# Routed expert blocks taken two at a time, and one tensor-engine event for each gather: a decoder layer on one Trainium2 core

## What is computed

```python
x = layernorm(x + attn(x))          # a state-space mixer with 32 heads
x = layernorm(x + xattn(x, ids))    # 4 experts, chosen by the token's id
x = layernorm(x + ffn(x))           # this is where the change is

def ffn(x):                         # 16 experts, top 2, and a shared one
    logits = x @ gate_w.T
    top_idx = top_k(logits + expert_bias, 2)
    w = softmax(logits)[top_idx]; w = w / sum(w)
    out = sum_k w_k * swiglu(x, expert top_idx_k)
    return out + swiglu(x, shared)
# swiglu(x, e) = (silu(x @ wg_e.T) * (x @ wu_e.T)) @ wd_e.T, inner width 176
```

## Time and profile before

| | |
|---|---|
| median of 3 runs | 666.92 us (666.61 to 666.98) |
| the profiled execution | 666.86 us |
| its span, first to last instruction | 665.1 us |
| mean granted TensorE clock | 0.985 |
| PE busy | 631.1 us, 95% of the span, 3545 matmuls |
| DVE, POOL, ACT busy | 531.7, 479.6, 453.6 us |
| routed blocks, 566.7 to 641.8 us | PE busy 71.2 us of 75.1 |
| end, 641.8 to 665.1 us | PE busy 4.6 us of 23.3 |

### The profile page before, as it was taken

The page is one execution under the profiler, slowest core; times in us unless marked ns, Lnnn a source line. Parts: engine busy times, 40 slices in busy tenths (PEclk is TensorE's granted clock), DMA queues, the critical chain, the costliest instruction groups (busy, mean ns, idle before and its releaser), DMA issues.

```text
span 665.1 us, 12037 instructions
## 1 busy us (share of the span) xinstructions
PE 631.1 (95%) x3545; PEld 489.1 (74%) x3545; DVE 531.7 (80%) x851; ACT 453.6 (68%) x739; POOL 479.6 (72%) x458
## 2 busy tenths in 40 slices
PE   7989999999999999999999999999999999899961
PEld 6677888888878888788888887878888877444530
DVE  6999999999999999999999999948952658323253
ACT  3769788797887887978879788776423455333534
POOL 4396989879879898798887987596914647854463
PEclk9999999999999999999999999999999999999995
DMA  4261113112121131111211212042063493577443
GB/s 161 88 253 49 65 49 111 63 48 75 42 106 63 48 111 63 48 63 48 111 63 48 88 47 87 0 128 101 16 164 87 109 306 147 156 234 235 100 118 112
DMA packets 25994, 66.67 MB, mean 100 GB/s; under 512 B 4099, under 2 KB 16899, under 8 KB 23179
## 3 DMA queue, kind: packets, MB, share of 16 engines
q1 hardware_dynamic: 23131, 58.54, 26.2%
q0 software_dynamic: 2832, 7.75, 4.4%
HBM read 58.00 MB, written 9.85 MB: 102 GB/s over the span
## 4 chain that ended last, share of the span: by engine, by line
PE 81%; DVE 7%; issue 3%; ACT 3%; POOL 2%; another core or an unknown queue 1%; DMA 1%; POOLq 0%; ACTq 0%; DVEq 0%
PE ps L874 36%; PE ps L888 9%; PE ps L904 7%; PE ps L889 4%; PE ps L1168 4%; DVE conv L1723 4%; PE ps L806 3%; PE ps L824 3%; PE ps L1217 3%; PE ps L848 2%; PE ps L913 1%; PE ps L1142 1%; PE ps L914 1%; PE ps L1192 1%
## 5 line engine op out<-in xcount | busy, mean ns | idle before, releaser
L1723 DVE SCALAR_TENSOR_TENSOR conv<-ps,w_raw,conv 128x506 f32<-128x506 f32 (+3 forms) x352 | 320.5, 933 | 14.8 <-ACT conv L1368 8.4
L874 PE MATMUL ps<-x_hi,w_hi 128*128 128x512 f32 x384 | 158.0, 412 | 2.6 <-DVE x_lo L1644 1.5
L1368 ACT ACTIVATE conv<-ps,w_raw 128x512 f32<-128x512 f32 x160 | 108.4, 688 | 63.7 <-PE ps L874 63.1
L874 PE MATMUL ps<-x_hi,w_lo 128*128 128x512 f32 x384 | 151.3, 394 | 0.0
L874 PE MATMUL ps<-x_lo,w_hi 128*128 128x512 f32 x384 | 150.1, 391 | 0.0
L528 POOL TENSOR_TENSOR decay<-cum_b,cum_tok 128x512 f32<-128x512 f32 (+1 forms) x128 | 103.4, 829 | 9.1 <-DMA cum_b<-cum_scratch 9.1
L874 PEld LDWEIGHTS ps<-x_hi,w_hi 128*128 128x128 f32 x384 | 72.3, 188 | 20.6 <-issue 2.4
L534 POOL TENSOR_TENSOR decay<-decay,mask 128x512 f32<-128x512 f32 x64 | 82.7, 1292 | 5.0
L874 PEld LDWEIGHTS ps<-x_hi,w_lo 128*128 128x128 f32 x384 | 72.1, 188 | 16.8 <-DVE w_lo L1649 0.2
L874 PEld LDWEIGHTS ps<-x_lo,w_hi 128*128 128x128 f32 x384 | 72.4, 189 | 12.7
L1353 ACT ACTIVATE conv<-conv 128x1024 f32<-128x1024 f32 x80 | 79.3, 1059 | 1.5 <-DVE conv L1723 1.5
(11 more groups left out here) (286 smaller groups left out, 1107.7 us busy)
## 6 DMA issues: line engine op xcount, KB each, us to landing
cum_b<-cum_scratch SPq DMA_DIRECT2D x16, 1024.0 KB, 4.6
w_raw<-in_winT SPq DMA_DIRECT2D x15, 778.0 KB, 4.3
y_all<-in_wgu SPq DMA_DIRECT2D x4, 1408.0 KB, 12.8
late<-in_wdn SPq DMA_DIRECT2D x2, 1408.0 KB
x_scratch<-conv SPq DMA_DIRECT2D x19, 128.0 KB, 4.9
late<-in_woutT SPq DMA_DIRECT2D x1, 2048.0 KB, 8.4
ys_scratch<-y_blk SPq DMA_DIRECT2D x32, 64.0 KB
res_scratch<-conv SPq DMA_DIRECT2D x11, 130.0 KB
```

Source lines behind the costliest of these rows:

```text
L874: mm = pe.matmul(ps[:, tile_bank(n, tile) + hf, :], wp[:, par, w], xp[:, kk, t], start=(i == 0), stop=(i == 5))
L1368: act.activation(conv[:, par, tile, hf * 512:(hf + 1) * 512], ps[:, tile_bank(n, tile) + hf, :], ACT.Copy, scale=w_raw[:, par, tap:tap + 1 ...
L1723: dve.scalar_tensor_tensor(out=o[:, :, s:], in0=u[:, :, 0:T - s], scalar=w_raw[:, par, c:c + 1], in1=o[:, :, s:], op0=ALU.mult, op1=ALU.ad ...
```

## The change

- PE takes routed items in pairs (i = 11, 13, ... 33): gate_up(i), gate_up(i + 1), down(i - 2), down(i - 1), turn_block(i + 2), turn_block(i + 3), turn_hidden(i), turn_hidden(i + 1). The first pair is laid out singly, since the shared items end inside it. ACT and DVE follow in the same order.
- POOL gathers the first 4 blocks freely. Of each further pair of blocks, the first waits for gate_up(i) of the pair four blocks earlier, the second for turn_hidden(i + 1) of it; from the second such pair on, one residual gather stands between them and waits for down(i - 2). The residual gathers are so spread over the pairs of blocks 6 to 20.
- The first six row gathers use the same three events in the last two pairs. The other ten wait for no event of PE.
- What hangs on the residual rows moves back with them: `SEEN_AT` by 6 items, `PICK_AT` by 4.
- At the end ACT normalises b = 0 to 4 and DVE b = 5 to 7, each one step behind the statistics of the next block; POOL normalises none. DVE's first weigh steps stand behind the last gate step, no longer between the last ones.

```diff
@@ -60,16 +60,15 @@
 RES = D + 4
-SEEN_AT = TBS + 11
-PICK_AT = TBS + 14
-LAST_ACT, LAST_POOL = 4, 6
+SEEN_AT = TBS + 17
+PICK_AT = TBS + 18
+LAST_ACT = 5
 HOISTED, LEADING = 3, 2
-BESIDE = 19
 PICK_PARTS = ((0, 0, HOISTED), (1, 0, LEADING), (0, HOISTED, TB), (1, LEADING, TB))
...
 NX = 8
-AHEAD = 3
+AHEAD = 4
 NSEL = 2
...
@@ -472,10 +471,8 @@
                     sp.wait_ge(S["n2a"], b + 1)
-                elif b < LAST_POOL:
-                    sp.wait_ge(S["n2p"], b - LAST_ACT + 1)
                 else:
-                    sp.wait_ge(S["n2"], b - LAST_POOL + 1)
+                    sp.wait_ge(S["n2"], b - LAST_ACT + 1)
                 sp.dma_start(out[b * P:(b + 1) * P, :], o_tok[:, b, :]).then_inc(S["st_out"], 16)
@@ -679,8 +676,6 @@
-                if j >= AHEAD:
-                    pool.wait_ge(S["tx_done"], j - AHEAD + 1)
                 pool.indirect_dma_start(xb[:, j % NX, :], None, x2_dram,
@@ -689,7 +684,6 @@
                     pool.wait_ge(S["st_res"], 16 * TBS)
-                    pool.wait_ge(S["gu_done"], TBS)
                 pool.indirect_dma_start(res_tok[:, b, :], None, res_dram,
@@ -716,27 +710,41 @@
             pool.wait_ge(S["v_tab"], 1)
-            for j in range(NBLK):
+            def in_pair(i, place):
...
+                if place == 0:
+                    pool.wait_ge(S["gu_done"], i + 1)
+                elif place == 1:
+                    pool.wait_ge(S["dn_done"], i - 1)
+                else:
+                    pool.wait_ge(S["ht_done"], i + 2)
...
+            for j in range(AHEAD):
                 gather_block(j)
...
                     add_residual(TBS - 4)
-                elif j == 4:
+            for j in range(AHEAD, NBLK, 2):
+                i = TBS + j - AHEAD
+                in_pair(i, 0)
+                gather_block(j)
+                if j == AHEAD:
                     add_residual(TBS - 3)
-                elif j == 5:
+                elif j // 2 - AHEAD // 2 <= TB:
+                    in_pair(i, 1)
+                    gather_res(j // 2 - AHEAD // 2 - 1)
+                in_pair(i, 2)
+                gather_block(j + 1)
+                if j == AHEAD:
                     add_residual(TBS - 2)
                     add_residual(TBS - 1)
-                if 7 <= j < 7 + TB:
-                    gather_res(j - 7)
...
             def beside_blocks(n):
-                j = BESIDE + min(n // 2, (n + 3) // 3)
-                if j < NBLK:
-                    pool.wait_ge(S["gu_done"], TBS + j + 1)
-                else:
-                    pool.wait_ge(S["dn_done"], ITEMS - 1)
+                if n < 6:
+                    in_pair(ITEMS - AHEAD + n // 3 * 2, n % 3)
@@ -752,10 +760,6 @@
                     gather_row(k, b)
-            for b in range(LAST_ACT, LAST_POOL):
-                pool.wait_ge(S["q2"], b + 1)
-                pool.tensor_scalar(o_tok[:, b, :], y_of[:, 0, b, :], ln_m2[:, b, 0:1], ln_v2[:, 1, b:b + 1],
-                                   ALU.subtract, ALU.mult).then_inc(S["n2p"], 1)
@@ -1290,21 +1294,35 @@
             turn_block(TBS)
-            for i in range(TBS, ITEMS + 2):
-                if i < ITEMS:
-                    gate_up(i)
+            for i in range(TBS, ITEMS, 2):
+                gate_up(i)
                 if i == TBS:
...
                     down(TBS - 1)
-                if i - 2 >= TBS:
+                gate_up(i + 1)
+                if i > TBS:
                     down(i - 2)
                 if i + 2 < ITEMS:
-                    turn_block(i + 2)
                     read_expert(i + 2 - TBS)
-                if TBS <= i - 1 < ITEMS:
-                    turn_hidden(i - 1)
+                if i > TBS:
+                    down(i - 1)
+                if i == TBS:
+                    turn_block(TBS + 2)
+                    turn_hidden(TBS)
+                    turn_block(TBS + 3)
+                    turn_hidden(TBS + 1)
+                else:
+                    if i + 2 < ITEMS:
+                        turn_block(i + 2)
+                        turn_block(i + 3)
+                    turn_hidden(i)
+                    turn_hidden(i + 1)
+                if i + 2 < ITEMS:
+                    read_expert(i + 3 - TBS)
+            down(ITEMS - 2)
+            down(ITEMS - 1)
@@ -1598,27 +1616,30 @@
             take_block(TBS)
-            for i in range(TBS, ITEMS + 2):
-                if i < ITEMS:
-                    silu_gate(i)
+            for i in range(TBS, ITEMS, 2):
+                silu_gate(i)
                 if i == TBS:
...
                     take_y(TBS - 1)
-                if i < ITEMS and i - 2 >= TBS:
-                    take_y(i - 2)
-                if i >= ITEMS:
-                    take_hidden(i - 2)
-                    if i == ITEMS:
-                        act.preload_act_table_set("natural_log_exp_and_others")
+                silu_gate(i + 1)
+                if i > TBS:
                     take_y(i - 2)
...
                     take_block(i + 2)
+                    take_block(i + 3)
+                if i > TBS:
+                    take_y(i - 1)
                 if i == PICK_AT:
...
                     act.preload_act_table_set("silu_and_others")
+            take_hidden(ITEMS - 2)
+            take_hidden(ITEMS - 1)
+            act.preload_act_table_set("natural_log_exp_and_others")
+            take_y(ITEMS - 2)
+            take_y(ITEMS - 1)
@@ -2059,26 +2080,27 @@
-            for i in range(TBS, ITEMS):
-                if i == ITEMS - 2:
-                    for b in range(HOISTED):
-                        weigh_low(b)
-                if i == ITEMS - 1:
-                    for b in range(LEADING):
-                        weigh_high(b)
+            for i in range(TBS, ITEMS, 2):
                 gate_block(i)
-                if TBS < i < ITEMS - 1:
-                    take_hidden(i - 1)
-                if i == SEEN_AT:
+                gate_block(i + 1)
+                if i + 2 < ITEMS:
+                    take_hidden(i)
+                    take_hidden(i + 1)
+                if i + 1 == SEEN_AT:
                     blocks_of_picks()
...
                     weights_of_picks()
+            for b in range(HOISTED):
+                weigh_low(b)
+            for b in range(LEADING):
+                weigh_high(b)
             for b in range(HOISTED, TB):
...
                 weigh_high(b)
-            for b in range(LAST_POOL, TB):
-                last_norm(b)
+                if b > LAST_ACT:
+                    last_norm(b - 1)
+            last_norm(TB - 1)
```

More of the change, by code:

```diff
@@ L275, in build_layer @@
                  "ld_sh ld_gu ld_dn ld_copy st_x2 st_res ld_res a_el "
-                 "tx_done a_xt gu_done a_s a_u p_h v_h ht_done a_ht v_ht dn_done a_y p_res v_mix st_out y_seen v_blk v_lb ys_set n2a n2p")
+                 "tx_done a_xt gu_done a_s a_u p_h v_h ht_done a_ht v_ht dn_done a_y p_res v_mix st_out y_seen v_blk v_lb ys_set n2a")
         S = {n: sem(n) for n in names.split()}
```

## The result

| | before | changed |
|---|---|---|
| median of the runs | 666.95 us (666.61 to 667.80, 4 runs) | 661.19 us (660.12 to 661.45, 4 runs) |
| ratio | | 0.990, 95% interval 0.988 to 0.992 |
| profiled execution / its span | 666.86 / 665.1 us | 660.12 / 658.4 us |
| PE busy | | 626.1 us (95%) |

The forecast was 660.6 us, within 658.0 to 666.5. The profiled execution is the fastest of the four; spans of the others are 659.4 to 659.7. In a later series the same kernel gave 0.992 (0.989 to 0.994).

What follows compares the result with a forecast made beforehand. PE bounds the kernel, busy everywhere but in the last 25 us. gate_up(33) starts at 576.9 + 52.9 + 0.7 + 0.8 + 1.5 = 632.8, last gather 650.8, plus 8.0 gives span 658.8, device time 660.6 us, range 658.0 to 666.5.

Steps and rivals of the forecast that it cites:

- PE's steps: Routed middle: PE's steps for a pair of items sum to 5.29 us against 5.58 before; 52.9 for ten pairs.
- handover: Between pairs: PE waits 0 to 0.1 us for turn and copy of the next block; 0.07 a pair, 0.7 for ten.
- late completions: Routed middle: PE completions seen late behind closely spaced POOL gathers; bounds 0 to 4.3 us, taken as 0.8 for ten pairs.
- late landings: Second gather of a pair landing after its rows' turn, 4.2 us behind its start; 0 to 7.5 us, taken as 1.5.
- What the middle had lost: Items 13 to 33 took 60.07 us instead of 55.8; the 4.3 was read as completions late behind close gathers.
- The end: From last row gather's start to span's end: 8.0 us where 13.4 stood before, a gain of 5.4.
- Before, these gathers could start earlier beside PE; that is the price of the change: Third part of row gathers: waiting for turn_hidden(34) counted as a cost, in the sum; POOL starts 5.2 us into that pair.
- ACT's fifth norm is hidden: At the end: norms come at 1.25 us and cost 1.5, so ACT is only 0.75 behind after b = 4.
- A residual gather holds up the turns: Rival, middle: completion behind the pair's middle gather 1.1 us late in 9 pairs, 9.9 in all; time 670.5; chance 0.11.
- Landings decide: Rival, middle: second gathers of five crowded pairs need 5.7 us, PE loses 7.5 instead of 1.5; time 666.6; chance 0.08.
- Only the end gains: Rival: completions still cost 4.3 us instead of 0.8 and SP's 2.2 wait at the end stays; 666.3; chance 0.04.
- No late landing: Rival, middle: second gathers land below 4.2 us, no turn waits, the 1.5 falls away; time 659.1; chance 0.15.

## Why the prediction was right, and where it was not

**PE's steps: right.** 5.29 a pair and 0.07 of handover were forecast, 5.35 to 5.36 came.

**Start and losses of the pairs: sizes off, sum right.** Item 13 starts at 578.13 instead of 576.9: the routed stage began 0.6 later in this execution, and the fourth gather landed after 4.61. From there handover, late completions and late landings were to cost 0.7 + 0.8 + 1.5 = 3.0 in ten pairs, and cost 54.68 - 52.9 = 1.8. The two errors cancel, which is luck: item 33 starts at 632.81, forecast 632.8.

**What the middle had lost: half right.** I gave all 4.3 to completions behind close gathers. 2.35 are shown to be the residual gathers'. From item 31 to item 33 the kernel before took 7.17 (629.52 to 636.69) instead of 5.58, 1.6 more, where row gathers stood 1.3 apart; that they are the cause there was not tried apart.

**Third part, last gather: right.** 638.12 and 650.82, forecast 638.0 and 650.8.

**The end: its terms right, the reason for the gain wrong.** The span ends 7.6 behind the last gather, forecast 8.0, and each term of that sum came within 0.2: 3.25 to DVE's last weighing (forecast 3.4), 1.15 for it (1.15), 0.60 for ACT's steps (0.55), 0.41 for the norm (0.6), and 2.2 from there to the end (2.25, of which 0.45 for the store and 0.4 at the end came from no row). Wrong was why it had been 13.4. The prediction named POOL's slower norms, the stores and the wait of 2.2. The step that failed reads "Before, these gathers could start earlier beside PE; that is the price of the change", together with "ACT's fifth norm is hidden". The wait is no price. Without it the gain is nil within the noise (0.999), since PE's completions come up to 8 us late beside gathers in a row, and ACT gets to its norms at 650.63 instead of 640.30. And the fifth norm is hidden only with ACT free at 640: in the single order it made DVE wait 4.09. The 5.4 of the end are not the norms': the pairs and waits with the old norms already have 0.993, about 5 of the 6 us. The new norms add 0.7 by the ratios, which is within the noise, and 2.2 by the end of the traces (9.8 against 7.6 behind the last gather), most of it the end of POOL's program. The new norms in the single order, with them the wait of the third part, and the new norms in pairs without the waits all gave 0.999. I had seen late completions in the earlier trace rows and used them for the middle only; ACT's rows from 644 to 651 would have shown them at the end.

**The rivals.** "A residual gather holds up the turns" is out at the distances of the change, 2.05 and 1.88, and is seen at 1.25. "Landings decide" did not decide, but is seen: a late landing and the clock behind it made single pairs of 6.4 to 7.2 in other executions. "Only the end gains" is out. "No late landing" is nearest to the trace of the ten pairs.

## What to carry to other kernels

Read every engine's last work at the end of a kernel, and not only the last transfer: an edit that shortens the last norms pays little while the engine that has to do them is kept by late events. Where POOL issues gathers in a row beside matmuls whose completion others wait for, give each gather an event of PE to wait for, and let the final burst begin behind the last completion that the critical path needs. An edit's parts can be worth nothing clear of the noise one by one and 5 to 6 us together, so take each part out of the whole, and not only add it to the old kernel, before you name the one that brought the gain.

## What the runs showed of the hardware

A completion of PE reached ACT about 8 us late (636.5, where `gate_up` of item 33 should end, to 644.61 in the kernel without waits) while POOL's gathers followed each other at 1.25; other completions in the same burst came through earlier (DVE at 636.79 and 639.63). In the change one was 0 to 0.7 late where two gathers stood 1.4 to 1.7 apart, and none behind a gather that stood 1.88 or more behind the one before. That the lateness goes with the distance between gathers is shown by the edits; how they do it, the traces don't say.

The granted clock fell to its lower level behind a PE wait of 3.7 us (0.50 at 649 in the kernel before) and behind one of 1.36 (0.56 from 608 on in the kernel with close residual gathers). At 0.50 the steps of `down` came 0.43 apart instead of 0.22. Behind waits of 0.54 and less, as in the change, it stayed at 1.00.

The span ended 5.1 to 5.2 us behind POOL's last operation in three kernels, whatever that operation was (658.84 to 664.0, 658.75 to 663.9, 659.96 to 665.1). So work on POOL that ends less than about 5 us before the end adds to the span, however small it is; this is read from these three.

A gather of 128 rows of 1 KB landed after 2.88 in a quiet part, after 4.61 in the first row of the chain above, and after 6.1 beside SP's weight copies. The Trainium skill, "DMA: Bandwidth & Descriptors", section "Anatomy of one DMA", gives an estimate of 2.3 by its fit; the quiet row is 0.6 above it, and the crowded one is far from it.
